# Next head's maxima in the present head, decoding spread over a head, weights turned by DMA

## What is computed

```python
xn = layernorm(x)
q, (k, v) = xn @ Wq, split(xn @ Wkv)          # 16 query heads, 4 key/value heads, head size 32
scores = q @ k.T / sqrt(32) + slope[head] * (s - t)   # causal
attn_out = softmax(scores) @ v @ Wo + bo
Wg, Wu, Wd = dequant(packed 4-bit codes, one scale per 32 columns)   # gate, up: 4096 x 512; down: 512 x 4096
g = xn @ Wg.T
ffn_out = ((tanh(0.79788 * (g + 0.044715 * g**3)) + 1) * g * 0.5 * (xn @ Wu.T)) @ Wd.T
out = x + attn_out + ffn_out
```

## Time and profile before

| | |
|---|---|
| median of 3 runs | 1727.42 us (1726.92 to 1729.85) |
| profiled execution | 1728.95 us, its span 1727.2 us |
| busy, share of the span | PE 96%, DVE 76%, ACT 62%, POOL 54% |
| mean granted TensorE clock | 0.995 |
| DMA | 106.86 MB, mean 62 GB/s |
| chain that ended last | PE 74%, DVE 8%, issue 6%, ACT 5% |

### The profile page before, as it was taken

The page is one execution under the profiler, slowest core; times in us unless marked ns, Lnnn a source line. Parts: engine busy times, 40 slices in busy tenths (PEclk is TensorE's granted clock), DMA queues, the critical chain, the costliest instruction groups (busy, mean ns, idle before and its releaser), DMA issues.

```text
span 1727.2 us, 30756 instructions
## 1 busy us (share of the span) xinstructions
PE 1664.6 (96%) x10337; PEld 830.8 (48%) x10337; DVE 1311.4 (76%) x2782; ACT 1067.2 (62%) x1788; POOL 935.4 (54%) x807
## 2 busy tenths in 40 slices
PE   5789999999999999999999999999999999999998
PEld 4664444444444444444444444444444444444443
DVE  7677777777777777777777777777777778777755
ACT  3337667575757667575757667575757657575650
POOL 3305547374655647374656647374656647364650
PEclk9999999999999999999999999999999999999999
DMA  7760110302020120202020120212020120212135
GB/s 221 190 194 24 41 49 17 79 23 76 24 73 17 46 57 17 76 26 76 23 73 17 45 57 17 76 27 76 22 75 17 39 64 17 76 27 83 31 103 182
DMA packets 95859, 106.86 MB, mean 62 GB/s; under 512 B 38304, under 2 KB 63784, under 8 KB 94008
## 3 DMA queue, kind: packets, MB, share of 16 engines
q1 hardware_dynamic: 91384, 99.27, 20.8%
q10 hardware_dynamic: 4320, 5.64, 1.0%
HBM read 69.60 MB, written 22.42 MB: 53 GB/s over the span
## 4 chain that ended last, share of the span: by engine, by line
PE 74%; DVE 8%; issue 6%; ACT 5%; DMA 0%; POOL 0%; SPq 0%; POOLq 0%; DVEq 0%; ACTq 0%
PE up_ps L1279 16%; PE down_ps L1259 16%; PE gate_ps L1279 15%; PE o_ps L1322 8%; PE score_ps L1313 8%; PE max_ps L1291 4%; PE turn_ps L1291 3%; ACT p L1441 2%; DVE mxp L1572 2%; PE l_ps L1322 2%; ACT wh L356 1%; PE max_ps L349 1%; DVE score_ps L1557 1%; DVE gl L1528 1%; DVE acc L1519 1%
## 5 line engine op out<-in xcount | busy, mean ns | idle before, releaser
L1714 POOL TENSOR_TENSOR plo<-p,phi 128x512 f16<-128x512 f32 (+1 forms) x576 | 661.0, 1158 | 318.0 <-ACT phi L1448 316.7
L1441 ACT ACTIVATE p<-score_ps,pshift 128x512 f32<-128x512 f32 (+1 forms) x576 | 381.8, 663 | 284.1 <-DVE score_ps L1557 154.6
L1448 ACT ACTIVATE phi<-p 128x512 f16<-128x512 f32 (+1 forms) x576 | 349.4, 607 | 15.3
L1722 POOL TENSOR_TENSOR il<-prod,ih 128x512 f16<-128x512 f32 x128 | 160.3, 1253 | 366.2 <-DVE ih L1551 366.2
L1313 PE MATMUL score_ps<-qst,kst 128*128 128x512 f32 (+3 forms) x640 | 308.4, 498 | 20.6 <-ACT p L1441 18.8
L1572 DVE TENSOR_REDUCE mxp<-max_ps 128x1 f32<-128x512 f32 x256 | 175.5, 686 | 52.3 <-PE max_ps L1291 52.3
L1519 DVE TENSOR_TENSOR acc<-down_ps,acc 128x512 f32<-128x512 f32 x237 | 161.8, 682 | 62.4 <-PE down_ps L1259 62.0
L1279 PE MATMUL gate_ps<-xh,wh 128*128 128x512 f16 x512 | 198.5, 388 | 0.0
L1279 PE MATMUL up_ps<-xh,wh 128*128 128x512 f16 x512 | 198.0, 387 | 0.0
L1259 PE MATMUL down_ps<-wh,ih 128*128 128x512 f16 x506 | 195.9, 387 | 0.0
L1279 PE MATMUL gate_ps<-xh,wl 128*128 128x512 f16 x512 | 194.7, 380 | 0.0
(11 more groups left out here) (313 smaller groups left out, 2851.5 us busy)
## 6 DMA issues: line engine op xcount, KB each, us to landing
qst<-q_parts SPq DMA_DIRECT2D x192, 64.0 KB
o<-oraw SPq DMA_DIRECT2D x192, 64.0 KB, 2.0
kst<-k_parts SPq DMA_DIRECT2D x45, 256.0 KB, 6.0
vst<-v_parts SPq DMA_DIRECT2D x16, 512.0 KB, 6.2
q_parts<-o SPq DMA_DIRECT2D x24, 256.0 KB, 3.1
raw<-L_ffn_gate_W_packed_dram SPq DMA_DIRECT2D x16, 256.0 KB, 3.0
raw<-n_L_ffn_up_W_packed_dram SPq DMA_DIRECT2D x16, 256.0 KB, 3.2
raw<-L_ffn_down_W_packed_dram SPq DMA_DIRECT2D x16, 256.0 KB, 3.9
```

What stands on the lines that cost most here:

```text
L1441: nc.scalar.activation(p32[n % PR][:, 0:cols], score_ps[:, 0:cols], ACT.Exp, bias=pshift[:, 0:1]).then_inc(exp_done, 1)
L1448: nc.scalar.activation(phi[n % PP][:, 0:cols], p32[n % PR][:, 0:cols], ACT.Copy).then_inc(phi_done, 1)
L1714: nc.gpsimd.tensor_tensor(plo[n % PP][:, 0:cols], p32[n % PR][:, 0:cols], phi[n % PP][:, 0:cols], ALU.subtract).then_inc(plo_done, 1)
L1722: nc.gpsimd.tensor_tensor(il[w % 2][:, a, :], prod[a][:], ih[w % 2][:, a, :], ALU.subtract).then_inc(il_done, 1)
```

## The change

The plan of a round becomes data (`Plan`, made by `plan`). The last 20 of the 40 maxima of a head stay in its own round; the first 20 (chunks 0 and 1 and the first 8 of chunk 2) run in the round before, at most one a slot. Scores stand in 36 of slots 0 to 43. Decoding runs in slots 8 to 12, 18 to 22 and 28 to 32. Round 0 has a plan of its own with 60 maxima; round 15 has 20.

The weights are no longer turned by TensorE. `rows_hi` (ScalarE) rounds `wf` to f16 rows in the space of the codes, `rows_lo` (GpSimd) writes the rest to a buffer of the outputs' parts, and SyncE turns both with two DMA transposes of 128x1024 f16 (`turn_rows`) straight into `wh` and `wl`: matrices 0 and 1 behind chunk 1's work in its queue, matrix 2 behind chunk 2's (all three behind chunk 2's in round 0). GpSimd's rows of one matrix wait for the transposes of the one before; the codes are loaded when the transposes are done. The down matrix's row scale moves into `product`'s scalar. The values are loaded once for the four heads that share them. Parts of `add_parts`, `row_sums` and `normalise` move to other slots. In the preamble the turns move to SyncE in the same way.

```diff
-MAX_PER_SLOT = [2, 2, 2, 2, 1, 2, 1] + [2, 1] * 4 + [2, 1] * 4 + [2, 1, 1]
-MAX_AT = [list(range(sum(MAX_PER_SLOT[:s]), sum(MAX_PER_SLOT[:s + 1]))) for s in range(SLOTS)]
-assert sum(MAX_PER_SLOT) == NMAX
-TURN_MAX_AT = {3: 0, 7: 1, 15: 2, 26: 3}
-SCORE_SLOTS = [s for s in range(6, SLOTS) if s - 1 not in TURN_MAX_AT][:NBLK]
-SCORE_AT = {s: n for n, s in enumerate(SCORE_SLOTS)}
-BLOCKS_BY_TURN = [sum(s <= turn for s in SCORE_SLOTS) for turn in TURN_MAX_AT]
-SLOT_OF = {n: s for s, n in SCORE_AT.items()}
+PV_INCS = 4
+W_DMAS = 2
...
-VALUES_AT = {SLOT_OF[blocks[-1]] + PV_LAG: b for b, blocks in enumerate(BATCHES)}
-assert max(VALUES_AT) < SLOTS
-PV_INCS = 4
-DECODE_FROM = {26: 0, 31: 1, 36: 2}
-DECODE_AT = {s + i: (m, i) for s, m in DECODE_FROM.items() for i in range(5)}
-DECODE_FIRST = min(DECODE_FROM)
-TURN_W_AT = {31: (0, 0), 32: (0, 1), 36: (1, 0), 37: (1, 1), 41: (2, 0), 42: (2, 1)}
-
-ROW_SUMS_AT = 14
-ADD_PARTS_AT, NORMALISE_AT, BIAS_AT = (19, 23), 36, 11
+EARLY = MAX_END[1] + 8
...
+def plan(max_slots, turn_at, score_slots, decode_from, turn_rows_behind):
+
+
+    maxima = [(0, n) for n in range(NMAX - sum(s < SLOTS for s in max_slots) + EARLY, NMAX)] + [(1, n) for n in range(EARLY)]
+    assert len(maxima) == len(max_slots) and len(score_slots) == NBLK
+    max_at = [[m for m, at in zip(maxima, max_slots) if at == s] for s in range(SLOTS)]
...
+    turn_after = {turn: sum(s < at for s in score_slots) for at, turn in turn_at.items()}
+    values_at = {min(score_slots[blocks[-1]] + PV_LAG, SLOTS - 1): b for b, blocks in enumerate(BATCHES)}
+    assert len(values_at) == NBATCH
+    decode_at = {s + step: (m, step) for m, s in enumerate(decode_from) for step in range(5)}
+    return Plan(max_at, turn_at, score_at, turn_after, values_at, min(decode_from), decode_at,
+                {s + 5: m for m, s in enumerate(decode_from)}, {s + 6: m for m, s in enumerate(decode_from)},
+                turn_rows_behind)
...
+MAX_PER_SLOT = [2, 2, 2, 2, 1, 2, 1] + [2, 1] * 4 + [2, 1] * 4 + [2, 1, 1]
+FIRST_PLAN = plan([s for s, count in enumerate(MAX_PER_SLOT) for _ in range(count)] + list(range(28, 48)),
+                  {4: (0, 0), 8: (0, 1), 16: (0, 2), 27: (0, 3), 33: (1, 0), 41: (1, 1)},
+                  without(range(6, 47), 8, 16, 27, 33, 41), (26, 31, 36), (2, 2, 2))
+EVEN_PLAN = plan(without(range(0, 22), 6, 13) + [23, 25, 26, 27, 28, 29, 31, 32, 34, 35, 37, 38] + list(range(40, 48)),
+                 {6: (0, 2), 24: (0, 3), 30: (1, 0), 40: (1, 1)},
+                 without(range(0, 44), 3, 6, 12, 18, 24, 30, 35, 40), (8, 18, 28), (1, 1, 2))
+
+ROW_SUMS_AT = 7
+ADD_PARTS_AT, NORMALISE_AT, BIAS_AT = (4, 6), 32, 11
...
-TURN_FIRST_AT = {(3, 0): 0, (3, 2): 1}
+ROWS_FIRST_AT = {(2, 4): 0, (3, 1): 1, (3, 4): 2}
+TURN_FIRST_AT = {(3, 1): 0, (3, 3): 1}
...
+    hi_rows = [t[:].bitcast(F16) for t in raw]
+    HALVES = (1, 1, 2)
...
+            sp.dma_start(raw[m][:].rearrange("p (a w) -> p a w", a=2), src.rearrange("o p a w -> (o p) a w")
+                         ).then_inc(raw_in[m], 16)
+            return
+        for a in range(2):
+            src = packed[2].rearrange("(k p) (g a w) -> g a p k w", p=P, a=2, w=GROUP // 4)[bass.ds(g, 1), a]
+            sp.dma_start(raw[m][:].rearrange("p (a k w) -> p a k w", a=2, k=KT)[:, a],
+                         src.rearrange("o p k w -> (o p) k w")).then_inc(raw_in[m], 16)
...
-                dve.wait_ge(wturn_done, before * 6 + 2 * m)
+                if m or before:
+                    dve.wait_ge(rowlo_done, before * 3 + m)
...
-    def turn_weights(pe, m, a, before, maxima):
-        pe.wait_ge(wf_done, before * 6 + 2 * m + 2)
-        if maxima is not None or 2 * m + a >= 2:
...
-        for k in range(KT):
-            at = a * C + k * P if m < 2 else k * GROUP + a * P
-            mm = nc.tensor.transpose(banks[a][:, k * P:(k + 1) * P], wf[:, at:at + P], ident[:])
-        mm.then_inc(wturn_done, 1)
...
-    def weights_hi(act, m, a, before, b):
-        act.wait_ge(wturn_done, before * 6 + 2 * m + a + 1)
-        if m == 2:
-            act.wait_ge(cur_done, before + 1)
-        nc.scalar.activation(wh[b][:, m, a, :], banks[a][:], ACT.Copy,
-                             scale=1.0 if m < 2 else cur[b][:, 4 + a:5 + a]).then_inc(wh_done, 1)
...
-    def weights_lo(dve, m, a, before, b):
-        dve.wait_ge(wh_done, before * 6 + 2 * m + a + 1)
-        nc.vector.scalar_tensor_tensor(wl[b][:, m, a, :], banks[a][:], 1.0 if m < 2 else cur[b][:, 4 + a:5 + a],
-                                       wh[b][:, m, a, :], ALU.mult, ALU.subtract).then_inc(wl_done, 1)
...
+    def rows_hi(act, m, before):
+        act.wait_ge(wf_done, before * 6 + 2 * m + 2)
+        nc.scalar.activation(hi_rows[m], wf[:], ACT.Copy).then_inc(rowhi_done, 1)
+
+    def rows_lo(pool, m, before, lo_row):
+        pool.wait_ge(rowhi_done, before * 3 + m + 1)
+        nc.gpsimd.tensor_tensor(lo_row, wf[:], hi_rows[m], ALU.subtract).then_inc(rowlo_done, 1)
+
+    def turn_rows(sp, m, before, b, lo_row):
+
+        for done, rows, dst in ((rowhi_done, hi_rows[m], wh[b]), (rowlo_done, lo_row, wl[b])):
+            sp.wait_ge(done, before * 3 + m + 1)
+            sp.dma_start_transpose(dst[:, m].rearrange("p a (k n) -> p (a k) n", n=P), rows).then_inc(w_in[m], 16)
+
+    return load_raw, decode_step, rows_hi, rows_lo, turn_rows
...
+                        if (c, j) in TURN_FIRST_AT:
+                            turn_rows(sp, TURN_FIRST_AT[c, j], 0, 0, lo_rows[TURN_FIRST_AT[c, j]])
...
+                turn_rows(sp, 2, 0, 0, lo_rows[2])
...
+                for m in range(3):
+                    rows_lo(pool, m, 0, lo_rows[m])
...
-                        if (c, j) in TURN_FIRST_AT:
-                            for a in range(2):
-                                turn_weights(pe, TURN_FIRST_AT[c, j], a, 0, None)
...
+                        if (c, j) in ROWS_FIRST_AT:
+                            rows_hi(act, ROWS_FIRST_AT[c, j], 0)
...
+        lo_rows = [o[:, 1, :].bitcast(F16) for o in o3]
...
-                body(i, i % 2, i // 2)
+                body(i, i % 2, EVEN_PLAN if i else FIRST_PLAN)
...
-                for m in range(3):
-                    load_raw(sp, m, 1)
-
-                def body(i, par, pair):
+
+                def body(i, par, plan):
                     nxt = (i + 1) % HEADS
-                    sp.wait_ge(pv_done, after(i * NBATCH * PV_INCS))
-                    load_v(i)
+                    if i % REP == 0:
+                        sp.wait_ge(pv_done, after(i * NBATCH * PV_INCS))
...
+                        for m in range(3):
+                            sp.wait_ge(w_in[m], 16 * W_DMAS)
+                            load_raw(sp, m, 1)
...
+                        for m, used in enumerate((gate_done, up_done, down_done)):
+                            if i < LAST and plan.turn_rows_behind[m] == c:
+                                sp.wait_ge(used, after(i * (GU if m < 2 else ND)))
+                                turn_rows(sp, m, i + 1, 1 - par, lo_rows[1 - par])
                     if i + 2 < HEADS:
                         for m in range(3):
-                            sp.wait_ge(wf_done, (i + 1) * 6 + 2 * m + 2)
+                            sp.wait_ge(w_in[m], 16 * W_DMAS * (i + 2))
                             load_raw(sp, m, i + 2)
...
+                                if n == 0:
+                                    pe.wait_ge(w_in[m], 16 * W_DMAS * (i + 1))
...
+                    def maximum(ahead, n):
+
+                        h = i + ahead
+                        if h == HEADS:
+                            return
...
+                        if n == 0:
+                            pe.wait_ge(k_in[h % 2], h // 2 * 48 + (48 if h % 2 else K_FIRST))
...
-                            pe.wait_ge(v_in, (i + 1) * 16)
+                            pe.wait_ge(v_in, (i // REP + 1) * 16)
...
-                    pe.wait_ge(k_in[par], pair * 48 + (K_FIRST if par == 0 else 48))
-                    pe.wait_ge(wl_done, (i + 1) * 6)
...
-                        if s in SCORE_AT:
...
+                        if s in plan.score_at:
+                            score(plan.score_at[s])
+                        if plan.max_at[s]:
+                            maximum(*plan.max_at[s][0])
...
+                        if s in plan.turn_at:
+                            turn_max(*plan.turn_at[s])
+                        if s in plan.values_at:
+                            values(plan.values_at[s])
+                        if len(plan.max_at[s]) > 1:
+                            maximum(*plan.max_at[s][1])
...
-                        if s in TURN_W_AT and i < LAST:
-                            m, a = TURN_W_AT[s]
-                            turn_weights(pe, m, a, i + 1, (red_done, after((i + 1) * NMAX)))
...
-                        if s - 1 in TURN_W_AT and i < LAST:
-                            m, a = TURN_W_AT[s - 1]
-                            if (m, a) == (0, 0):
...
```

(25 more changed lines are left out.)

181 lines of the change are left out of this document (84 added, 97 removed).

## The result

The changed kernel takes 1716.95 us (median of 4 runs, 1716.47 to 1718.14), the kernel before beside it 1728.49 us (1726.92 to 1729.85). The ratio is 0.9935, with a 95% interval of 0.9917 to 0.9952: faster by 11.5 us, where 17 were forecast. The profiled execution took 1716.76 us.

What follows compares the result with a forecast made beforehand. TensorE was taken to set the pace. Heads 1 to 14 -15.4, head 0 +3, head 15 -7.6 and preamble +3 make -17; 1728.95 - 17 - 1.5 = 1710 us, own range 1695 to 1724, 8 in 10 1662 to 1756.

Steps and rivals of the forecast that it cites:

- the four places: Parts of the forecast sum: heads 1 to 14 -15.4 us, head 0 +3, head 15 -7.6, preamble +3.
- TensorE's groups: Six groups of weight transposes a head, 0.44 us each, leave TensorE: -2.6 us in each of 15 heads.
- Waits: TensorE's waits in a middle head: 5.7 us after the change against 4.2 before, mostly from moved decoding.
- Slot 22: Its causal addition waits behind accumulate, reduce, four small reduces, gelu and the fourth decoding step: 1.85 us lost.
- Slots 10 and 15: Decoding in slots 8 to 12 delays exponentials: 1.3 us lost at slot 10, 1.05 at 15.
- The new plan: Decoding moved beside the maxima costs waits, +1.5 us a middle head; spreading maxima one per slot saves no matmul.
- decoding harmless: Rival: decoding does not hurt, waits fall to about 3 us a head, 1668 us; chance 0.24.
- Last head: Head 15: 20 fewer maxima, -3.7 us; without decoding its waits fall from about 6.4 to 2.5; together -7.6.
- Preamble: SyncE must also wait for matrix 2's rows, then two issues: +3 us, between -1 and +8.
- Head 0: 20 more maxima +3.7 us, weight groups -2.6, decoding meeting borrowed maxima +2: together +3.
- The queue: Rival: transposes hold SyncE's queue, delaying slot 28's row-sum copy; 1752 us at 4.1 us each; chance 0.17.

Runs made afterwards that it cites:

- old_plan: Against the kernel before: its old slots in all heads, no borrowed maxima, only the change's crossbar transposes kept; 1747.28 us, ratio to before 1.0108.
- last_sums14: Changed kernel, but in the last head alone VectorE reduces the row sums in slot 14 instead of 7; 1708.62 us, ratio 0.9890.
- up_at_22: Changed kernel with up matrix decoded in slots 22-26, last head's row sums in 14, Wo maxima in 12, 15, 18, 19, preamble gate transposes earlier; 1695.19 us.
- first_turns: Changed kernel, but in the preamble SyncE issues the gate matrix's transposes one store earlier; 1714.17 us.
- tiny_decode: Changed kernel, but from the second matrix set on each decoding step works on 32 of 512 columns; 1700.35 us.

## Why the prediction was right in sign and off in its terms

The total, 1710 against 1717, is close by luck: the four places miss by +12.6, -4.6, -3.0 and -9.8 us and cancel in part.

*TensorE's groups, -2.6 a head.* As work this was right to 0.01 us a slot. As a gain it failed: the step took 0.44 us off the path six times without asking who would then be waited for. old_plan shows 0.75 us a head lost, and slot 33 of the last head of before, where the groups are absent, had shown a part of it.

*Waits, 5.7 against 4.2.* The terms of the prediction add up to 6.0, not 5.7. Measured are 5.7, but by the same count before had 4.7, so the growth was 1.0 and not 1.5; and -2.6 + 1.0 leaves 0.4 of the measured -2.0 that the count does not place. Slot 22 was right in size and mechanism: priced at 1.85, 1.77 measured, of which 1.17 are decoding steps. In all, decoding makes at least 1.4 us of a head, not the 4.5 or so that I charged to it. Slots 10 and 15 came out at 0.47 and 0.15 instead of 1.3 and 1.05, where the steps took 2.9 us and not 4.4: the mis-sized term is the mean of the earlier trace rows, most of whose steps began while GpSimd worked. Slots 0, 6 and 30 (1.3 together) were not foreseen.

*The new plan.* I priced it as a loss that the transposes pay for. It is the other way round: transposes alone +0.75 us a head, the plan on top of them -2.75 (98.14 to 95.39). The plan without the transposes was not run, so how much of its gain is only their loss undone is open. The rival "decoding harmless" did not hold either: it had waits of 3 us a head, and took the 2.6 for granted, as the forecast did.

*Last head, -7.6 forecast, +2.2 measured.* The largest miss at the ends, 10 us. I had counted the row sums' move nowhere: SyncE's queue in the last head was not looked at, though the change moves VectorE's wait seven slots forward. The tail, some 3 us shorter than before's in this execution, hides a part. From the head's first MLP matmul to its last the times are 104.4 before, 109.4 after, 102.5 in last_sums14 and 98.5 in up_at_22, where the maxima of Wo stand elsewhere too; 96.8 was forecast. So the row sums cost some 6.8 us. The move of Wo's maxima out of slots 17 to 20 gave another 4.0, of which 1.7 in slots 23 and 24, where last_sums14 had the lower clock.

*Preamble, +3 forecast, +7.6 measured.* The two issues at the end were counted, the transposes ahead of the stores only named as what would make it wrong. first_turns gives 4.5 back.

*Head 0, +3 forecast, +6.0 measured.* Decoding and borrowed maxima meet in slots 33 to 41; tiny_decode gives back 3.5 us, where I had 2 for the decoding. And the 2.6 of the weight groups were not there either: with the transposes alone (old_plan) head 0 took 97.0 against 96.8.

*The queue.* The rival in which the transposes hold it is out: they land in 3 us, and the copies behind them did not wait. How much longer they could take without cost was not measured.

## What to carry to other kernels

Work taken off the bounding engine is a gain only where that engine does not then wait; look for a stretch of the same trace in which that work is absent (here the last head) and read who is waited for there. Treat first and last iterations as places of their own: of 28 us won in the middle, 16 were lost at the ends, about two thirds of that by SyncE issues that stood ahead of a small transfer somebody needed. A step costs what stands behind it: two decoding steps ahead of one causal addition cost 1.17 us a head in slot 22, and in slots 22 to 26 the steps of the same matrix made none of these slots longer. And a run that makes an operation small does not take it away: 32 columns took 0.75 us and 512 columns 0.77, since both stood beside GpSimd. Read the operation's own time in the trace before the result is called its cost.
